# Key loads of an attention kernel: upper row half issued by GpSimd, lower by the sync engine

## The reference, cut to what matters

```python
qh = _split_heads(q @ Wq + bq); kh = _split_heads(k @ Wk + bk); vh = _split_heads(v @ Wv + bv)
logits = jnp.einsum('bhsd,bhtd->bhst', qh, kh) / jnp.sqrt(DEPTH)      # 16 heads, 1024 x 6404
out = jnp.einsum('bhst,bhtd->bhsd', jax.nn.softmax(logits, axis=-1), vh)
```

## Time and profile before

| | us |
|---|---|
| median of 3 runs | 873.7 (872.42, 873.7, 881.33) |
| profiled execution | 870.89 |
| its span | 869.2 |
| ACT, PE, DVE, POOL busy | 738.2, 719.9, 689.8, 169.0 |
| mean granted TensorE clock | 0.953 of full speed |

### The profile page before, as it was taken

The page is one execution under the profiler, slowest core; times in us unless marked ns, Lnnn a source line. Parts: engine busy times, 40 slices in busy tenths (PEclk is TensorE's granted clock), DMA queues, the critical chain, the costliest instruction groups (busy, mean ns, idle before and its releaser), DMA issues.

```text
span 869.2 us, 38041 instructions
## 1 busy us (share of the span) xinstructions
PE 719.9 (83%) x15210; PEld 321.5 (37%) x15212; DVE 689.8 (79%) x1952; ACT 738.2 (85%) x650; POOL 169.0 (19%) x304
## 2 busy tenths in 40 slices
PE   6987678878899889879997899699878998899851
PEld 3435334423443344324433343233323443344331
DVE  3428749975999699939995999589958996899866
ACT  2446779997999999969997999799979997999842
POOL 2502412211222122202220222112211221122100
PEclk9999789998999999989999999999999999999965
DMA  3213321111111111111111111111111111111000
GB/s 104 77 55 115 126 82 35 33 42 40 36 34 40 40 36 36 40 39 37 35 38 41 36 35 36 44 36 35 35 44 37 35 35 44 37 34 35 23 1 25
DMA packets 31714, 38.38 MB, mean 44 GB/s; under 512 B 3534, under 2 KB 30192, under 8 KB 31616
## 3 DMA queue, kind: packets, MB, share of 16 engines
q1 hardware_dynamic: 30748, 36.57, 13.9%
q10 hardware_dynamic: 868, 0.48, 0.2%
HBM read 30.15 MB, written 6.42 MB: 42 GB/s over the span
## 4 chain that ended last, share of the span: by engine, by line
SPq 28%; ACT 25%; issue 18%; PE 17%; DMA 6%; DVE 5%; POOL 1%; ACTq 1%; POOLq 0%; DVEq 0%
SPq L290 24%; ACT probs L708 23%; PE ps L1312 7%; DMA k_op<-k_parts_dram 4%; PE ps L1282 3%; SPq L306 2%; PE ps L1211 2%; PE ps L1197 2%; SPq L503 1%; DMA k_parts_dram<-k_parts 1%; DVE stats L774 0%; POOL k_parts L539 0%; PE ps L1160 0%; DMA q_parts_dram<-q_parts 0%; DVE probs L1091 0%
## 5 line engine op out<-in xcount | busy, mean ns | idle before, releaser
L708 ACT ACTIVATE probs<-ps 128x1536 f32<-128x1536 f32 (+1 forms) x536 | 673.9, 1372 | 48.4 <-PE ps L1282 47.3
L1312 PE MATMUL ps<-probs,v_op 64*9 64x512 f32 (+1 forms) x8384 | 528.0, 503 | 48.2 <-DMA k_op<-k_parts_dram 42.2
L1282 PE MATMUL ps<-q_op,k_op 59*32 59x512 bf16 x6432 | 344.0, 386 | 52.0 <-ACT probs L708 42.5
L977 DVE SCALAR_TENSOR_TENSOR e_u<-e_u,e_f 128x256 f32<-128x256 f32 x720 | 259.6, 426 | 0.0
L1282 PEld LDWEIGHTS ps<-q_op,k_op 59*32 59x32 bf16 x6432 | 114.9, 91 | 318.7 <-issue 240.8
L1312 PEld LDWEIGHTS ps<-probs,v_op 64*9 64x9 f32 x8384 | 166.0, 87 | 139.0 <-issue 50.7
L958 DVE TENSOR_SCALAR e_t<-ps 128x256 f32<-128x256 f32 x240 | 90.7, 419 | 105.2 <-PE ps L1282 96.8
L586 POOL TENSOR_SCALAR e_pow<-e_t 128x512 int32<-128x512 int16 x120 | 74.3, 619 | 364.7 <-DVE e_t L958 364.7
L579 POOL COPY v_op<-v_all 128x108 f32<-128x108 f32 x136 | 62.6, 460 | 215.0 <-PE ps L1312 214.3
L977 DVE SCALAR_TENSOR_TENSOR e_u<-e_f 128x256 f32<-128x256 f32 x240 | 90.1, 417 | 0.2
L984 DVE SCALAR_TENSOR_TENSOR probs<-e_u,e_pow 128x256 f32<-128x256 f32 x240 | 89.6, 411 | 0.0
(11 more groups left out here) (177 smaller groups left out, 247.1 us busy)
## 6 DMA issues: line engine op xcount, KB each, us to landing
k_op<-k_parts_dram SPq DMA_DIRECT2D x544, 24.0 KB
k_op<-k_parts_dram SPq DMA_DIRECT2D x272, 36.0 KB
k_parts_dram<-k_parts SPq DMA_DIRECT2D x17, 288.0 KB, 2.8
ctx_nat<-in_ctx_dram SPq DMA_DIRECT2D x16, 192.0 KB, 2.6
q_op<-q_parts_dram SPq DMA_DIRECT2D x32, 32.0 KB
q_parts_dram<-q_parts SPq DMA_DIRECT2D x2, 384.0 KB, 3.8
q_op<-q_parts_dram SPq DMA_DIRECT2D x16, 48.0 KB
x_nat<-in_x_dram SPq DMA_DIRECT2D x1, 512.0 KB, 3.7
```

Source lines behind the costliest of these rows:

```text
L708: act.activation(probs[:, b % NP].rearrange("p u t -> p (u t)")[:, 0:columns], ps[:, bank:bank + BU, :].rearrange("p u t -> p (u t)")[:, 0 ...
L977: dve.scalar_tensor_tensor(out=e_u[:, cols], in0=u[:, cols], scalar=a, in1=e_f[:, cols], op0=ALU.add, op1=ALU.mult).then_inc(e_step, 1)
L1282: return pe.matmul(ps[a:a + P // G, bank, :], k_op[W2 * r:W2 * r + KR, kslot, i, P * j + a:P * j + a + P // G], q_op[W2 * r:W2 * r + KR, q ...
L1312: last = pe.matmul(ps[32 * k:32 * k + DH + 1, ACC[h], a:b], v_op[W2 * h:W2 * h + W2, slot, j, (DH + 1) * k:(DH + 1) * (k + 1)], probs[W2 * ...
```

## The change

`load_k` gets a parameter `halves`. SP now issues only the half r = 0 of each key load (chunks 0 to 2 of the first phase are still loaded whole by SP); POOL issues the half r = 1, three DMAs, in `load_second(m)` ahead of `stage` of chunk m, for the chunk m + 3, once the scores of chunk m - 1 are done. It signals semaphores of its own, `k_second_loaded`, and PE waits for both. POOL's code is written out for all 136 chunks, so its addresses and counts are constants. Ahead of its first chunk POOL waits until all the key parts are written.

```diff
+        k_second_loaded = [sem(f"k_second_loaded{i}") for i in range(KS)]
...
-        def load_k(sp, slot, chunk, group, signal, counter=None, count=None):
+        def load_k(sp, slot, chunk, group, signal, counter=None, count=None, halves=range(R2)):
...
-            starts = [sp.snap(src.offset + r * (rows * CK)) for r in range(R2)]
+            starts = {r: sp.snap(src.offset + r * (rows * CK)) for r in halves}
...
-            for r in range(R2):
+            for r in halves:
...
             for c in range(1, KS):
-                load_k(sp, c, c, slice(0, 32), k_loaded[c], k_parts_written[c], 16)
+                load_k(sp, c, c, slice(0, 32), k_loaded[c], k_parts_written[c], 16,
+                       range(R2 if c < KS - 1 else 1))
...
                     load_k(sp, slot, chunk, slice(32 * group, 32 * group + 32), k_loaded[slot],
-                           scores_done, before + AHEAD)
+                           scores_done, before + AHEAD, range(1))
...
+            def load_second(m):
+
+                ph, c = divmod(m + KS - 1, NC)
+                slot, g = (m + KS - 1) % KS, ph % NG
+                load_k(pool, slot, c, slice(32 * g, 32 * g + 32), k_second_loaded[slot], scores_done,
+                       m // NC * BPP + m % NC * BPC + AHEAD, range(1, R2))
+
+            pool.wait_ge(scores_done, AHEAD)
+
+            for slot in range(4):
+                pool.wait_ge(k_parts_written[slot], 16 * len(range(slot, NC, 4)))
             for ph in range(PHASES):
                 for c in range(NC):
                     m = ph * NC + c
+                    if m <= PHASES * NC - KS:
+                        load_second(m)
                     stage(m % 2, m, c * CT, ph % NG * G)
...
-                        wait(k_loaded[(m + 1) % KS], at(K_LOAD * ((m + 1) // KS + 1), K_LOAD // KS))
+                        n, half_load = (m + 1) // KS, K_LOAD // R2
+                        n += (m + 1) % KS == KS - 1
+                        wait(k_loaded[(m + 1) % KS], at(half_load * ((m + 1) // KS + 1)
+                                                        + half_load * ((m + 1) % KS < KS - 1), half_load // KS))
+                        if n:
+                            wait(k_second_loaded[(m + 1) % KS], at(half_load * n, half_load // KS))
```

## The result

The kernel after takes 836.07 us (median of 4 runs, 834.99 to 837.98), the kernel before 873.35 us in the same comparison: ratio 0.9563, 95% interval 0.951 to 0.9615, 4.4% faster. The forecast was 841 us. The profiled execution took 836.67 us with a span of 834.9, 34.3 us under the span before.

A forecast was written before the change was run, and what follows sets the result against it. SP's DMA issue queue was taken as the bound. Start +7.9, rest of phase 0 -1.0, its end -5.2, six phases -31.6, phase 7 0: -29.9 from 870.9 gives 841 us; forecast's own range 830 to 852, wider range 830 to 918.

The forecast's parts named there:

- The bound: SP's queue issuing key DMAs: 5.0 us per chunk against 4.95 for other engines, no reserve for the phase's end.
- The phase: Each of six phases between ACT's first operations of phases 1 and 7: 89.7 us falls to 84.4, together -31.6 us.
- the wait for the accumulators: At each turn PE waits for DVE to empty the accumulators: 0.8 us, untouched by the change.
- phase 7: The last phase, with no phase behind it: gain counted as 0.
- PE's second wait: Extra wait after block 2 of each chunk: costed at nothing, hidden by 0.30 us waiting for ACT; 20 us if uncovered.
- POOL's price: Time one DMA holds POOL, called d: taken as 1.0 us, ends 0.6 and 2.35; POOL's chunk 4.4 us.
- The start: Phase 0: POOL's first copy waits for all stores, PE's values start 12.6 us late; net +7.9 us after old holes vanish.
- Rival 1: POOL becomes the bound, slower: a POOL DMA above 1.32 us makes PE wait every chunk; 917 us at 1.4; chance 0.30.
- the formula: POOL's time per phase, 22.5 + 51d us with d for one DMA: 73.5 at 1.0; POOL takes over from 1.21.
- the copy's 0.52 us beside DVE: Sign that POOL's work suffers beside DVE: its copy takes 0.28 us while DVE stands, 0.52 beside DVE's operations.
- Rival 3: DVE's emptying of the accumulators holds the turn, so relieving SP wins nothing and the start costs: 882 us; chance 0.04.
- the two-port rule: DVE in a two-port mode keeps GpSimd from writing descriptors: phase of 181 us; 3 in 100, inside the POOL-bound rival.

The follow-up runs named there:

- experiment 1: Kernel before, with SP's loop over key loads written out so every address is constant and POOL issuing no DMAs: 829.61 us, ratio 0.9502.
- experiment 7: Kernel after, with PE's wait for the second key half issued four times instead of once, repeats always fulfilled: 835.58 us, ratio 0.954.
- experiment 3: Kernel after, with POOL issuing all six key DMAs of a chunk and SP only those of the first four chunks: 847.15 us, single execution.
- experiment 8: Kernel after, POOL's first copies moved ahead of its wait for the stores, plus three unused fp32 SBUF copies on DVE per phase except the first: 825.92 us.

## Why the prediction was right, and where it was off

**The bound.** "A queue that others wait for and that waits for nobody" held: experiment 1 frees SP with no other edit and gets the same 587 us for seven phases.

**The phase.** 84.4 us was forecast, 83.9 measured. The term that was off is the wait for the accumulators, put at 0.8 us per turn, PE's mean wait; ACT loses about 0.4 to it (chunk 1 takes 5.76 us where 5.34 were counted). From ACT's first operation of phase 1 (199.89) to that of phase 7 (703.43) six phases change by -34.5 us, where -31.6 was forecast; phase 7, put at no gain, changes by -1.0. These two make up most of the 4.3 us between 841.0 and the profiled 836.7.

**PE's second wait at nothing.** Right, with more room than the 0.3 us named: experiment 7.

**POOL's price.** The term that was mis-sized most: d = 1.0 us against 0.577 measured. It lay outside even the lower end of 0.6, which had been taken from SP's fastest DMA, on the belief that POOL can't be quicker. It moved no result, as POOL stayed hidden either way. The Trainium skill (DMA: Bandwidth & Descriptors, section Specifications) has the slower first byte on GpSimd's side; for the time that an issue holds its engine, these rows say the opposite, 0.577 against 0.655.

**The start.** Forecast +7.9 us for the two holes, -1.0 for the rest of phase 0 and -5.2 for its end, +1.7 in all, for ACT's first operation of phase 1; it moved from 198.68 to 199.89, +1.2. That is close partly by luck: the cross-attention began 2.0 us later (103.97 against 101.98), which is not the change's, since experiment 1, with POOL's program as before, begins at 103.5; phase 0 itself became 0.8 us shorter. The hole came as worked out: PE's first values at 119.59 against 119.1, with the stores landed at 117.0 rather than 115.6 and POOL's three DMAs at 1.9 us rather than 3.0. But ACT's idle stretch was 11.58 us against the 13.6 counted for PE and the cold clock.

**Rival 1.** Its mechanism is real and its point was set wrongly. By the formula the loss begins where three DMAs take 3.6 us in a chunk; experiment 3 has 3.42 us of DMAs in a chunk and already loses 10.6 us in seven phases, for the gaps of 2.2 us and the copies of 2.65 us that the formula does not have. What I named as a sign for it, the copy's 0.52 us beside DVE, was read rightly for the copy and does not hold for the DMAs. In the kernel before, all 111 copies that begin while DVE runs an operation e_u<-e_u,e_f end 0.13 to 0.14 us after a DVE operation ends, and 98 of them outlast two (0.49 to 0.58 us); the 23 that begin while DVE stands or reads PSUM for acc_sb take 0.27 to 0.28. At the median the copy starts there 0.05 us ahead of one operation's end, when the next has already begun; after the change it starts 0.17 us ahead, when the next has not, so 102 of 109 outlast only one, and the mean falls from 460 to 353 ns. POOL's DMAs show nothing of the kind: the 215 of the kernel after that begin under the same operations all take 0.55 to 0.59 us.

**Rival 3** (the turn held by something else) fell with ACT's unbroken run through the turns. For the two-port rule of the Trainium skill inside rival 1 (SBUF — State Buffer, section SBUF: two separate sides) the copies of experiment 8 give no support in the half microsecond of overlap that they had, and can't refute it.

## What to carry to other kernels

A queue that issues DMAs has a budget like an engine's: multiply its issues per stage by its price, register work included, and compare with the bound engine's time for the stage; it is full when it hardly ever waits for what releases its loads. Before part of its work goes to another engine, try to make it cheaper where it is: addresses made constant by writing the loop out gave the whole gain here. When work is put into another engine's program, look at what stands behind its first wait; nine microseconds of this change's gain were lost there. And leave that engine more room than the sum of its operations asks for: experiment 3 fitted by its sum and still lost 10.6 us.

## What was not expected of the hardware

- A DMA issued by POOL held POOL for a median of 0.577 us, one by SP held SP for 0.655 us (0.637 in experiment 1). Cut from 24 or 16 rows to 8, it still took 0.518: nearly all of the price doesn't depend on the rows.
- POOL's 399 DMAs made 25536 packets, 64 each; the same DMAs from SP made 30748 - 22369 = 8379, 21 each. They took 6.2% of the span of 834.9 us on each of the 16 engines, 52 us, against 39 us for the same loads from SP (13.9% of 869.2 less 9.8% of 834.9), for 11.5 to 11.6 MB. It cost nothing here, where the DMA engines are at 15% (window of 204 to 700 us).
- In the kernel before, every copy of v_op on POOL that started under DVE's operations e_u<-e_u,e_f ended 0.13 to 0.14 us after a DVE operation's end: 0.52 us at the median, against 0.28 with DVE idle. In experiment 3 three copies that started just ahead of them took 2.65 us, to the end of the last.
- The Trainium skill (DMA: Bandwidth & Descriptors, section Issuing engines are not separate DMA queues) says that issuing from several engines saves only the time that the sequencer takes to initiate a DMA, usually small beside the DMA itself. Experiment 1 agrees with the first half, since without a second queue the same is reached. For the second, one issue with its register work is 0.833 us beside a landing of 2.91 us; what decided here is their sum, 5.0 us of issues in a chunk of 4.95 us.
